# A fused attention and feed-forward kernel: attended values moved ahead of the narrow block's transposes

## The reference

```python
x = x + 0.5 * ffn(layernorm(x), w_gate, w_up, w_down)      # silu(gate) * up, hidden 384
# attention on layernorm(x):
h = silu(x @ W1.T + b1) @ W2.T + b2
q, k, v = split(h @ Wg.T + bg)                             # 16 heads of 64
dots = einsum('bhid,bhjd->bhij', q, k) * 64 ** -0.5
dots = where(j >= i + 64, -inf, dots)
out = einsum('bhij,bhjd->bhid', softmax(dots), v)
x = x + out @ Wo.T + bo
x = x + 0.5 * ffn(layernorm(x), w_gate, w_up, w_down)
```

## Time and profile before

| what | value |
|---|---|
| median of 3 runs | 1325.9 us (1325.73 to 1326.67) |
| the profiled execution | 1328.12 us, of which the span is 1326.3 us |
| PE busy | 1263.1 us, 95% of the span |
| POOL busy | 1156.3 us, 87% |
| DVE busy | 935.0 us, 70% |
| ACT busy | 846.8 us, 64% |
| granted clock of TensorE, mean | 0.994 |

### The profile page before, as it was taken

One profiled execution on the slowest core, in us unless ns is written; L12 is line 12 of the kernel. 1 busy time (PEld: TensorE's weight loads), 2 busy tenths in 40 slices (PEclk: granted clock), 3 DMA queues, 4 the chain that ended last, 5 costly groups with the idle time before them and its releaser, 6 DMA issues.

```text
span 1326.3 us, 35410 instructions
## 1 busy us (share of the span) xinstructions
PE 1263.1 (95%) x11374; PEld 1003.3 (76%) x11374; DVE 935.0 (70%) x2120; ACT 846.8 (64%) x1896; POOL 1156.3 (87%) x1090
## 2 busy tenths in 40 slices
PE   4987999999999999999999999999999999999988
PEld 3765777777777777777777777777777777777777
DVE  4866776777776777777776776777776777776755
ACT  3455666667666666666666666666666667666632
POOL 6837899999999999999999999999999999999983
PEclk9998999999999999999999999999999999999999
DMA  4231122112211111112112211111111112110001
GB/s 138 114 119 61 64 66 65 42 61 64 64 64 64 64 59 32 62 64 64 41 62 64 64 64 64 64 59 32 62 64 64 42 61 64 64 64 7 8 17 48
DMA packets 80961, 80.22 MB, mean 60 GB/s; under 512 B 38049, under 2 KB 65314, under 8 KB 80930
## 3 DMA queue, kind: packets, MB, share of 16 engines
q1 hardware_dynamic: 80930, 79.82, 18.5%
HBM read 47.13 MB, written 8.39 MB: 42 GB/s over the span
## 4 chain that ended last, share of the span: by engine, by line
PE 68%; issue 13%; DVE 9%; ACT 5%; POOL 2%; SPq 1%; DVEq 1%; DMA 1%; ACTq 0%; POOLq 0%
PE banks L986 18%; PE banks L1003 15%; PE banks L964 15%; PE banks L890 5%; DVE negmax L729 5%; PE banks L944 3%; PE banks L855 3%; PE banks L1008 3%; ACT probs L545 2%; DVE banks L724 2%; PE banks L885 2%; PE banks L847 2%; PE banks L848 2%; ACT qt L467 2%; POOL probs L448 1%
## 5 line engine op out<-in xcount | busy, mean ns | idle before, releaser
L448 POOL TENSOR_SCALAR probs<-probs,recips 128x256 f32<-128x256 f32 (+7 forms) x512 | 882.1, 1726 | 106.2 <-DVE recips L734 106.1
L545 ACT ACTIVATE probs<-banks,negmax 128x320 f32<-128x320 f32 (+7 forms) x512 | 399.9, 788 | 66.7 <-DVE negmax L729 56.9
L553 ACT ACTIVATE probst<-banks 128x512 f32<-128x512 f32 (+2 forms) x512 | 266.0, 545 | 276.1 <-PE banks L986 276.1
L729 DVE TENSOR_REDUCE negmax<-banks 128x1 f32<-128x320 f32 (+7 forms) x512 | 393.9, 811 | 32.0 <-PE banks L964 4.2
L986 PE MATMUL banks<-ident,probs 128*128 128x128 f32 x2304 | 331.2, 280 | 1.9 <-DVE probst L741 1.3
L964 PE MATMUL banks<-kt,qt 64*128 64x512 f32 (+4 forms) x2496 | 302.1, 368 | 32.4 <-ACT probs L545 32.4
L986 PEld LDWEIGHTS banks<-ident,probs 128*128 128x128 f32 x2304 | 250.6, 141 | 82.3 <-issue 74.6
L1003 PE MATMUL banks<-probst,vs 128*64 128x128 f32 (+1 forms) x3328 | 279.8, 319 | 0.1
L964 PEld LDWEIGHTS banks<-kt,qt 64*128 64x128 f32 x2496 | 191.9, 186 | 95.0 <-ACT probs L545 52.0
L1003 PEld LDWEIGHTS banks<-probst,vs 128*64 128x64 f32 x3328 | 202.5, 137 | 72.4 <-issue 22.8
L450 POOL TENSOR_SCALAR ends<-probs,recips 128x64 f32<-128x64 f32 x448 | 198.6, 443 | 0.0
(11 more groups left out here) (71 smaller groups left out, 1039.5 us busy)
## 6 DMA issues: line engine op xcount, KB each, us to landing
xth<-h_split SPq DMA_DIRECT2D x62, 512.0 KB, 4.1
hslot<-h_sb SPq DMA_DIRECT2D x32, 512.0 KB, 3.1
wsplit<-w_split SPq DMA_DIRECT2D x31, 256.0 KB, 4.5
vh<-vs SPq DMA_DIRECT2D x64, 112.0 KB, 2.3
h_split<-qt SPq DMA_DIRECT2D x16, 256.0 KB, 2.2
w_split<-kt SPq DMA_DIRECT2D x4, 512.0 KB, 3.8
wslot<-in_wqkvt SPq DMA_DIRECT2D x32, 64.0 KB, 2.5
y<-xres SPq DMA_DIRECT2D x8, 256.0 KB, 2.3
```

The source lines that it names most:

```text
L448: last = nc.gpsimd.tensor_scalar(here, here, recips[:, c, h:h + 1], None, ALU.mult)
L545: nc.scalar.activation(probs[c][:, h, :], src, ACT.Exp, bias=negmax[:, c, h:h + 1], accum_out=sums[:, c, h:h + 1]).then_inc(exped.sem, 1)
L553: nc.scalar.activation(probst[c // 2 % 2][:, 4 * g:4 * g + w, c % 2 * P:(c % 2 + 1) * P], banks[:, TRANSPOSED[g % 2], 0:w * P].rearrange(" ...
L729: nc.vector.tensor_reduce(negmax[:, c, h:h + 1], rows[:, h, 0:hi], AX.X, ALU.max, negate=True).then_inc(maxed.sem, 1)
```

## The change

In odd steps that attend, PE multiplies by the values right behind the scores, and transposes and projects after that. ScalarE takes its exponentials first, then copies the attended values, then copies all its transposed groups, also groups 0 and 1. Steps that do not attend keep their order, and so do VectorE, POOL and SP.

```diff
--- before.py
+++ after.py
@@ -564,15 +564,16 @@
                 ti, tc = back(i, c, T_LAG)
                 turning = carry or c >= T_LAG
                 mine = [g for g in range(groups[tc]) if turning and taker(tc, g) == 0]
-                for g in mine:
-                    if g < 2:
+                attending = c in ATTEND_AT and (carry or c >= PV_LAG)
+                if not attending:
+                    for g in mine:
+                        if g < 2:
+                            take(tc, g, ti)
+                exps(c, i)
+                if attending:
+                    attention_out(ATTEND_AT[c], i if c >= PV_LAG else i - 1)
+                    for g in mine:
                         take(tc, g, ti)
-                exps(c, i)
-                if c in ATTEND_AT and (carry or c >= PV_LAG):
-                    for g in mine:
-                        if g >= 2:
-                            take(tc, g, ti)
-                    attention_out(ATTEND_AT[c], i if c >= PV_LAG else i - 1)
                 job = JOBS.get(c, "none")
                 if job[0] in "kq" and runs(job, carry, more):
                     queries_keys(job, job_turn(job, i), 1 - r if job_turn(job, 0) else r)
@@ -1021,6 +1022,8 @@
                 attending = c in ATTEND_AT and (carry or c >= PV_LAG)
 
                 score(c, i, r)
+                if attending:
+                    attend(ATTEND_AT[c], *((i, r) if c >= PV_LAG else (i - 1, 1 - r)))
                 if turning:
                     turns_of(tc, ti, (0, 1))
                 job = JOBS.get(c, "none")
@@ -1034,8 +1037,6 @@
                     project(job, job_turn(job, i), 1 - r if job_turn(job, 0) else r)
                 if turning and attending:
                     turns_of(tc, ti, (2, 3))
-                if attending:
-                    attend(ATTEND_AT[c], *((i, r) if c >= PV_LAG else (i - 1, 1 - r)))
                 if c in OUTPUTS and runs(OUTPUTS[c], carry, more):
                     output(OUTPUTS[c], job_turn(OUTPUTS[c], i))
                 if turning and not attending:
```

## The result

The changed kernel takes 1346.14 us (median of 4 runs, 1345.69 to 1347.31), the kernel before 1326.29 us beside it (4 runs, 1325.73 to 1328.64): ratio 1.0149, 95% interval 1.0134 to 1.0164. It is slower by 19.9 us. The forecast was 1347, with 1325 to 1357 as its range.

The account below looks back on a forecast made before the run. PE bounds the kernel at 98%, with 0.72 us of waits a turn. Stalls of 0.26 + 0.38 + 0.02 = 0.66 us over 31 turns (20.5) plus 0.8 give 21.3 more, 1347 on the medians' scale; range 1325 to 1357.

Parts of the forecast that it names:

- Step 7 into 0: Step 0's first transposes wait for ScalarE's copy of group 0 from step 7: 0.26 us a turn, bounds 0.15 to 0.40.
- step 1: The ninth transpose waits for ScalarE's copy of group 0: 0.38 us a turn, bounds 0.25 to 0.55.
- The sign that was named in advance: New PE waits before step 1's ninth and step 0's first transposes, 0.3 to 0.4 us, 31 each; scores' waits unchanged.
- Steps 3 and 5: Into step 4, a stall of 0.02 us a turn (0 to 0.15); into step 6, 0 (-0.05 to +0.15).
- VectorE, POOL, SP: Step 1's products start 1.1 us later, over 3.2 in hand; SP's value halves still fit by 0.8: no cost.
- a change of the kind of matmul: Each change costs PE about 0.1 us; as many changes as before, so 0, between -0.2 and +0.2 a turn.
- Step 6: At its start the query copy comes at about the same time: priced at 0, between -0.05 and +0.15 us.
- the tail: The last step 7 runs on with no scores between: 0.8 us, once.
- B: Faster: masks and maxima run faster beside the values, so exponentials end earlier; 1303.6 without stalls, half 1315; chance 0.10.
- A: No change: the copies are in time because ScalarE's instructions run closer together; 1325.9; chance 0.08.
- C: POOL's products come late by more than 3.2 us and PE waits in odd steps: 62 more, about 1388; chance 0.03.
- D: The clock falls to 1.2 GHz in the transposes from 606.96 to 610.27: 102 us more, about 1430; chance 0.03.

Follow-up runs that it names:

- e2_only_step7: The new order of PE and ScalarE in step 7 alone, against the kernel before: 1333.2 us, ratio 1.0053.
- e4_copy_before_attended: The changed kernel, with ScalarE copying groups 0 and 1 before the attended values: 1336.77 us, ratio 1.0075 against the kernel before.
- e3_only_steps_3_5: The new order in steps 3 and 5 only, the old one in steps 1 and 7, against the kernel before: 1326.86 us, ratio 1.0000.
- e7_takers_swapped: The changed kernel, with VectorE and ScalarE trading their groups of the narrow blocks: 1332.05 us, ratio 1.0047 against the kernel before.
- e5_scalar_keeps_order: PE in the changed order, ScalarE in the order of the kernel before (copies of groups 0 and 1 ahead of exponentials): 1586.14 us in one run.

## Why the prediction was right

**The bound.** PE was read as the bound with 0.72 us a turn to win and every new wait to lose. That held: every engine had the same work, PE's new waits were forecast to make the turn 0.66 us longer, and it is 0.64 longer in one turn and 0.647 over 31.

**Step 7 into 0 and step 1.** 0.26 and 0.38 were forecast, 0.25 and 0.41 read in one turn, 0.20 and 0.46 in the kernels that move only one step, 0.20 and 0.45 over all turns of the changed one. The chain of four distances behind the last sum record came out within 0.02 us. The forecast was worked out from one turn and fits that kind of turn; over all turns one term is 0.06 too large and the other 0.07 too small, and that they cancel in the sum is luck. The sign that was named in advance holds in part: the wait in front of step 0's transposes shows at the matmuls in every second turn only (14 times in 200 to 1200 us of e2_only_step7), though in each turn at the weight loads (28). What the forecast missed in step 1 is that the ninth transpose, once it has waited, takes 0.26 us to the next scores (623.34 to 623.60) and not 0.20: a start with nothing ahead of it in PE. For step 0 the forecast named ScalarE's order alone; e4_copy_before_attended shows the second limit 0.12 us below, which the forecast did not need and did not see.

**Steps 3 and 5.** Forecast 0.02 and 0; e3_only_steps_3_5 has 0.10 us in all 31 turns. One thing there was not foreseen: the scores of step 4 wait 0.45 us now and not 0.24, so the list of waits grew from 20.0 to 24.9 us where the forecast had said unchanged. PE comes there sooner: before, the value projection's weight loads waited for the keys' low half (4.5 us in 27 waits), and this wait is gone from the list. But the exponentials end when they did (they start 3.64 us behind the scores of step 3 in both traces), so a gain of PE was turned into idle time at once.

**VectorE, POOL, SP.** In step 1 the reciprocal came 6.54 us behind the scores and not 5.33, 1.2 later (forecast 1.1), and POOL's idle time before those products rose from 1.40 to 2.53 us. No wait of PE for POOL is in the list. That this delay costs nothing was argued in the forecast; e7_takers_swapped bears it out. POOL had more in hand than the forecast said: the 6.89 us of the earlier trace rows are three products, of which the third is step 2's, and those of step 1 end 5.67 us behind 615.97, at 621.64, 4.4 us before PE wants them. SP issued the value halves 6.31 us behind the scores of step 3 and not 5.71, 0.6 later (forecast 0.8), and PE has no wait for a transfer there. One reading was too general: a change of the kind of matmul does not cost 0.1 us each time, for in step 5 before, the projection starts 0.03 us behind the last transpose (631.18 and 631.15). It was priced at 0 and nothing came of it.

**Step 6.** It is 0.04 us shorter (0.03 over all turns), which the forecast had at 0 within its bounds: ScalarE's query copy starts 0.34 us behind the scores and not 0.40.

**The ends.** The forecast added 0.8 us for the tail, and it came. Behind the last step 7 the next transposes now wait for the copy,

```profile
1275.94 1.06 PE L987 MATMUL banks<-ident,probs 128*128 128x128 f32 x8 [0.67 <-ACT probst L553]
```

and from the last step 7's scores to them it is 5.42 us, before 4.67. Yet the whole tail, from the last step 7 to the end, is shorter: 73.4 us and 74.3 before. The change is not what shortens it. The next attended values and the few matmuls behind them, 1262.29 to 1266.28 us in the kernel before and 1281.55 to 1283.88 in the changed one, were granted different clocks (columns as in the tables of stretches above: PEclk is the third number from the end):

```profile
1262.29:1266.28 3.99, 3.99 (x33) 3.21 (x32) 0.15 (x1) 0.28 (x1) 3.77 (x5) 0.57 0.00 0
```

```profile
1281.55:1283.88 2.33, 2.33 (x34) 1.88 (x33) 0.16 (x1) 0.28 (x1) 2.03 (x4) 1.00 0.00 0
```

That is 1.66 us which the profiled execution of the kernel before lost by the clock. It does not come from the old order: e3_only_steps_3_5 has it in step 7 too, and the 24 matmuls there take 1.96 us, as in the changed kernel, where the kernel before took 3.50. With the start of the first step 7, 1.6 us earlier, this makes 17.6 us of span out of 20.05 in the turns. That the medians differ by 19.9 is as near as their own spreads, 2.9 and 1.6 us, allow.

**The rivals.** B (faster) fell with its premise: beside the values VectorE is no faster than beside the transposes. In step 3 its mask takes 0.49 us and its maxima 2.22 in both traces, in step 6 0.42 and 1.42. A fell with the two waits, C with the lack of any for POOL. D, the lower clock, did not come with transposes side by side: PEclk is 1.00 from 600 to 680 us of the changed kernel's trace too. The Trainium skill ("TensorE: Matmul & The Clock Gate", Part 4) says that transposes do not count as other matmuls do; nothing here shows such an effect. From 200 to 1200 us the clock fell only in e5_scalar_keeps_order, behind long waits.

## What to carry to other kernels

When a block of work moves in one engine's queue, look for every buffer it fills, and ask when its reader is done now and who wants the buffer next: here two banks with six tenths of a microsecond between two uses. A reader that is moved behind another instruction (here the copies behind the exponentials) costs nothing only while its buffer is not wanted; here that could be worked out to a few hundredths of a microsecond from the timeline before. And look at the busiest engine's remaining waits before reordering it: the change moved work in four places, none of which touched the 0.72 us that there was; two smaller moves aimed at it won 0.25 us a turn.

## What was not expected of the hardware

PE's granted clock fell to 0.62 over 4.5 us (617.70 to 622.24) in e5_scalar_keeps_order, with PE busy 84% of the time (334.48 of 400 us), behind single waits of 1.77 and 1.52 us; the longest in the trace from 200 to 1200 us is 2.3. In all other kernels here, with single waits of at most 0.5 us there, it was 1.00 from 200 to 1200 us. In the tail the clock differed behind nearly the same waits: behind waits of 1.27 and 0.34 us the kernel before was granted 0.57 over 4.0 us (1262.29 to 1266.28), and the changed kernel, behind waits of 1.33 and 0.34, 1.00 at the same place. Why was not found.
